# Twelve residual blocks on one core: where residual sums are made, who feeds the scan, how queries are folded

## The reference

```
x  += l0x cross attention (16 heads of 8)          block 1
x  += selective scan of l0a (16 states)            block 2
x  += l0f: 2 of 8 experts                          block 3
x  += l1x cross attention with one key head        block 4
x  += l1a causal self attention                    block 5
x  += l1f: base + one picked adapter               block 6
x  += l2x cross attention over 2048 keys           block 7
x  += norm(l2a gated linear recurrence) * gamma + beta   block 8
x  += l2f: 1 of 16 experts with capacity 40        block 9
x  += norm(l3x: 16 heads of 64, normed q and k, a null key) * g   block 10
x  += l3a self attention, norm, Wfc                block 11
x  += l3f: shared and 4 of 16 experts              block 12
```

## Time and profile before

| | us |
|---|---|
| median of 3 runs | 1161.91 (1161.63 to 1162.94) |
| the profiled execution, its own time | 1163.65 |
| its span, first to last instruction | 1161.9 |
| PE busy | 1075.1 |
| DVE busy | 576.2 |
| ACT busy | 427.0 |
| POOL busy | 312.9 |

### The profile page before, as it was taken

The page is one execution under the profiler, slowest core; times in us unless marked ns, Lnnn a source line. Parts: engine busy times, 40 slices in busy tenths (PEclk is TensorE's granted clock), DMA queues, the critical chain, the costliest instruction groups (busy, mean ns, idle before and its releaser), DMA issues.

```text
span 1161.9 us, 14452 instructions
## 1 busy us (share of the span) xinstructions
PE 1075.1 (93%) x5446; PEld 607.2 (52%) x5446; DVE 576.2 (50%) x1023; ACT 427.0 (37%) x709; POOL 312.9 (27%) x96
## 2 busy tenths in 40 slices
PE   6998798998899889889799999999999999999778
PEld 4554335665744455768564444544454445443654
DVE  2897783236477662344454434444443344343444
ACT  2665513316488633422252233222322332223111
POOL 0000000000000000000016666566746675566000
PEclk9999989988899999999999999999999999999999
DMA  8300000030000020240000000000000000000200
GB/s 334 137 1 1 1 1 1 1 145 1 3 1 1 10 101 1 84 188 1 1 1 18 19 18 20 17 19 18 19 14 19 19 22 14 18 18 5 80 1 10
DMA packets 21372, 40.08 MB, mean 34 GB/s; under 512 B 2496, under 2 KB 18880, under 8 KB 19648
## 3 DMA queue, kind: packets, MB, share of 16 engines
q1 hardware_dynamic: 21312, 39.25, 9.2%
HBM read 38.98 MB, written 0.26 MB: 34 GB/s over the span
## 4 chain that ended last, share of the span: by engine, by line
PE 81%; DVE 10%; ACT 5%; issue 2%; POOL 1%; DMA 0%; POOLq 0%; DVEq 0%; ACTq 0%
PE PSUM L2112 19%; PE PSUM L2116 18%; PE PSUM L1540 10%; PE PSUM L1816 3%; PE PSUM L1827 2%; PE PSUM L1601 2%; PE PSUM L1506 1%; PE PSUM L2023 1%; PE PSUM L1626 1%; PE PSUM L2244 1%; PE PSUM L2159 1%; POOL RSTD L384 1%; PE PSUM L1610 1%; DVE ARENA L985 1%; DVE ST L800 1%
## 5 line engine op out<-in xcount | busy, mean ns | idle before, releaser
L441 POOL TENSOR_TENSOR ARENA<-ARENA 128x2048 f32<-128x2048 f32 x64 | 289.0, 4516 | 175.5 <-ACT ARENA L726 175.5
L1354 DVE TENSOR_TENSOR ARENA<-PSUM,RK 128x512 f32<-128x512 f32 x256 | 175.9, 691 | 280.4 <-PE PSUM L2112 278.5
L2116 PE MATMUL PSUM<-ARENA,CK 128*128 128x512 f32 x512 | 251.2, 593 | 2.1 <-ACT ARENA L726 2.1
L2112 PE MATMUL PSUM<-ARENA,CK 128*128 128x512 f32 x512 | 251.3, 593 | 0.7 <-ACT ARENA L722 0.7
L726 ACT ACTIVATE ARENA<-ARENA,CK 128x2048 f32<-128x2048 f32 x64 | 128.1, 2002 | 311.6 <-DVE ARENA L1354 311.6
L2116 PEld LDWEIGHTS PSUM<-ARENA,CK 128*128 128x128 f32 x512 | 96.7, 190 | 126.4 <-issue 107.9
L2112 PEld LDWEIGHTS PSUM<-ARENA,CK 128*128 128x128 f32 x512 | 96.0, 190 | 117.9 <-issue 96.3
L384 POOL TENSOR_TENSOR RSTD<-VE,MHALF 128x4 f32<-128x4 f32 x15 | 15.1, 1009 | 437.6 <-DVE VE L808 437.6
L1540 PE MATMUL PSUM<-WK,CT 128*128 128x512 f32 x256 | 126.1, 615 | 0.1
L829 DVE TENSOR_REDUCE RK<-SQ 128x8 f32<-128x512 f32 x128 | 84.4, 682 | 28.2 <-ACT SQ L471 27.0
L1513 PE MATMUL PSUM<-WA 128*128 128x128 f32 x584 | 80.8, 293 | 13.3 <-DVE VE L808 10.0
(11 more groups left out here) (395 smaller groups left out, 1199.6 us busy)
## 6 DMA issues: line engine op xcount, KB each, us to landing
CT<-in_ctxT SPq DMA_DIRECT2D x4, 1024.0 KB, 10.3
CK<-in_l0f_experts SPq DMA_DIRECT2D x1, 4096.0 KB, 22.8
CK<-in_ctxk SPq DMA_DIRECT2D x1, 4096.0 KB, 12.5
ARENA<-in_l2f_experts SPq DMA_DIRECT2D x2, 2048.0 KB, 8.9
CK<-in_ctxT SPq DMA_DIRECT2D x64, 64.0 KB, 1.8
CK<-in_ctxr SPq DMA_DIRECT2D x64, 64.0 KB, 1.9
ARENA<-in_l2f_experts SPq DMA_DIRECT2D x1, 3072.0 KB, 14.3
WB<-in_wb SPq DMA_DIRECT2D x1, 2834.5 KB, 11.1
```

Of the source, the lines that this page charges most:

```text
L441: nc.gpsimd.tensor_tensor(LS[b % 2], LS[b % 2], PR[:, k % 2, :], ALU.add)\
L1354: ve.tensor_tensor(PR[:, k % 2, c * 512:(c + 1) * 512].rearrange("p (j n) -> p j n", j=4), PSUM[:, c % 2, :].rearrange("p (j n) -> p j n", ...
L2112: mm(bank(c % 2), CTT[:, k, :], qpb[:, b, c * 512:(c + 1) * 512], start=True, stop=True)\
L2116: return mm(bank(4 + c), CKT[:, k, :], PR[:, k % 2, c * 512:(c + 1) * 512], start=first, stop=final, skip_group_check=True)
```

## The change

1. **Residual sums in the bank.** `put_x_pe` multiplies X by the identity into the output bank, and the block's last products are added on it, in blocks 1, 2, 4, 5, 6 and 11. `norm_dve` reads its statistics from the bank, ACT then copies the bank to X (`keep_x_act`) and signals `x_ready`. The lift of block 1 stands in the heads loop at head 12. Block 3 adds the experts straight to X.
2. **Scan.** For the groups 1 to 3, ACT copies the spread rows of B to SBUF and POOL multiplies them by DTU; two input buffers in place of one; the spreads are in another order.
3. **Start.** An exponential of four numbers stands first on ACT; PE runs four idle products before the first transpose and three of four key groups of the first batch before the queries.
4. **Block 4.** Idle products stand in three more places. In other places their number is lower: after a block's end 4 for 6 before the variance, 5+9 and 6+9 for 6+12 around an output norm, 7 for 11 in block 8, 5 for 9 in block 11.
5. **Norms of outputs** (blocks 8 and 10) are fused with gain and sum into eight instructions, four before and four after POOL's power; block 8's output bias goes into the bank by PE. Blocks 7 and 11 divide and add in four instructions for two.
6. **Last attention, start.** The fold has 8 steps of 8 products in which the two halves of the array's rows alternate, with four pairs of banks; ACT copies one bank and DVE the other. The null scores of batches 1 and 2 stand in the first four key tiles.
7. **Last attention, between batches and end.** The null values are made before they are needed, and added in the midst of the fourth tile's scaling. For the last batch the first eight heads' values are made ahead of the sum over partitions, and the null values are added ahead of the division's denominator.

```diff
@@ scan block: addresses, GpSimd
-        CONV, U, VG, DT, DTU, ZB, EB1 = (ARENA[:, 640 + k * 512:1152 + k * 512] for k in range(7))
+        CONV, ZB, EB1, U, VG, DT, DTU = (ARENA[:, 640 + k * 512:1152 + k * 512] for k in range(7))
-        DBU = ARENA[:, 9472:9472 + 2048]
+        DBU = (ARENA[:, 9472:9472 + 2048], ARENA[:, 0:2048])
+        INPUTS_AT, READS_AT = (0, 4, 12, 20), (8, 16, 24, 28)
             for q in range(4):
+                if q == 1:
+                    nc.gpsimd.wait_ge(sem("l0a_bc_taken"), 1)
+                if q:
+                    for n in range(4):
+                        nc.gpsimd.wait_ge(sem("l0a_b_kept"), PO.due("l0a_b_kept"))
+                        at = DBU[q % 2][:, n * 512:(n + 1) * 512]
+                        nc.gpsimd.tensor_tensor(at, at, DTU, ALU.mult).then_inc(sem("l0a_input"), PO.sends("l0a_input"))
                 nc.gpsimd.wait_ge(sem("l0a_decay"), PO.due("l0a_decay"))
...
@@ ScalarE
+            def keep_x_act(k):
+                nc.scalar.wait_ge(sem("x_counted"), AC.due("x_counted"))
+                act(X[:, :, :].rearrange("p b n -> p (b n)"), bank(k), ACT.Copy).then_inc(sem("x_ready"), AC.sends("x_ready"))
...
+            nc.scalar.wait_ge(sem("halves"), 1)
+            act(SM[:, 1016:1020], MHALF[:, :], ACT.Exp)
             nc.scalar.wait_ge(sem("dma_wa"), AC.due("dma_wa"))
             turn_act(HT)
...
             for q in range(4):
-                due = AC.due("l0a_scan", lag=2)
-                ...
+                if q >= 2:
+                    nc.scalar.wait_ge(sem("l0a_scan"), q - 1)
+                if q:
+                    for n in range(4):
+                        k = INPUTS_AT[q] + n
+                        nc.scalar.wait_ge(sem("l0a_bc"), k + 1)
+                        act(DBU[q % 2][:, n * 512:(n + 1) * 512], bank(SPREAD_BANKS[k % 6]), ACT.Copy)\
+                            .then_inc(sem("l0a_b_kept"), AC.sends("l0a_b_kept"))
...
             for b in range(B):
-                for j in range(4):
+                for j in range(2):
                     nc.scalar.wait_ge(sem("l3x_qp"), AC.due("l3x_qp"))
-                    act(qph[:, b, j // 2, j % 2:8:2, :], bank4(j % 2), ACT.Copy)...
+                    act(qph[:, b, j, 0:8:2, :], bank4(2 * ((2 * b + j) % 4)), ACT.Copy)...
@@ VectorE: norms
-            def norm_dve(src, turned=True, twice=False):
+            def out_norm_dve(src, gain, number):
+                count_dve(src)
+                variance_dve()
+                for b in range(B):
+                    last = ve.scalar_tensor_tensor(out=HN[:, b, :], in0=src[:, b, :], scalar=MV[:, b, 0:1], in1=gain,
+                                                   op0=ALU.subtract, op1=ALU.mult)
+                ...
+                nc.vector.wait_ge(sem("rstd"), DV.due("rstd"))
+                for b in range(B):
+                    last = ve.scalar_tensor_tensor(out=X[:, b, :], in0=HN[:, b, :], scalar=RSTD[:, b:b + 1], in1=X[:, b, :],
+                                                   op0=ALU.mult, op1=ALU.add)
+                last.then_inc(sem("x_ready"), 1)
+            def norm_dve(src, turned=True, twice=False, summed=None, number=0):
+                if summed is None:
+                    count_dve(src)
+                else:
+                    nc.vector.wait_ge(sem("block_out"), DV.due("block_out"))
+                    count_dve(bank4(summed), "x_counted")
+                variance_dve(twice)
+                if summed is not None:
+                    nc.vector.wait_ge(sem("x_ready"), number)
                 nc.vector.wait_ge(sem("rstd"), DV.due("rstd"))
...
-            def tail_dve():
-                nc.vector.wait_ge(sem("block_out"), DV.due("block_out"))
-                ve.tensor_tensor(X[:, :, :], X[:, :, :], bank4(7), ALU.add).then_inc(sem("x_ready"), DV.sends("x_ready"))
...
             for h in range(H):
+                if h == 12:
+                    nc.vector.wait_ge(sem("dma_consts"), DV.due("dma_consts", n=4))
+                    lift_dve(row("l0x_bo"))
...
-            tail_dve()
-            norm_dve(X, twice=True)
+            norm_dve(X, twice=True, summed=7, number=1)
...
@@ VectorE: scan block
-                for n in range(4):
-                    ve.tensor_tensor(DBU[:, at:at + 512], bank(SPREAD_BANKS[(q * 8 + n) % 6]), DTU, ALU.mult)...
+                if q == 0:
...
+                else:
+                    nc.vector.wait_ge(sem("l0a_input"), 4 * q)
...
@@ VectorE: last attention
-            for b in range(B):
-                null_scores(b)
+            null_scores(0)
+            null_scores(3)
+            for b in range(B):
+                for j in range(2):
+                    nc.vector.wait_ge(sem("l3x_qp"), DV.due("l3x_qp"))
+                    ve.tensor_copy(qph[:, b, j, 1:8:2, :], bank4(2 * ((2 * b + j) % 4) + 1))...
             for b in range(B):
                 for k in range(DEEP):
-                    scale(b, k, k)
+                    scale(b, k, k, values_first=b > 0 and k == 3)
+                    if b == 0:
+                        null_scores(1 + k // 2, k % 2)
...
             keep_z(B - 1)
+            null_values(B - 1)
+            add_null_values()
             finish_sums(B - 1)
             finish_values()
             finish_out(B - 1)
-            norm_dve(OAT, turned=False)
-            ve.tensor_tensor(ACC[:, :, :], HN[:, :, :], over(row("l3x_go"), B), ALU.mult)...
-            ve.tensor_tensor(X[:, :, :], X[:, :, :], ACC[:, :, :], ALU.add)...
+            out_norm_dve(OAT, row("l3x_go"), 10)
@@ TensorE
+            def put_x_pe(k):
+                mm(bank(k), ident, X[:, :, :].rearrange("p b n -> p (b n)"), start=True, stop=False, skip_group_check=True)
-            def tail_pe(weight, src=OT):
+            def tail_pe(weight, src=OT, on_x=True):
                 for b in range(B):
+                    ... start=not on_x, stop=True, skip_group_check=on_x)
...
+            stay_busy(4, 1)
             turn_pe()
+            nc.tensor.wait_ge(sem("dma_ctx0"), PE.due("dma_ctx0"))
+            for g in range(1, 4):
+                key_pieces(g, 0)
             nc.tensor.wait_ge(sem("turned_kept"), PE.due("turned_kept"))
...
+            put_x_pe(7)
             turn_pe(ACC)
...
+            spread_inputs(0)
+            stay_busy(2, 1)
+            spread_inputs(1)
+            stay_busy(4, 1)
+            spread_reads(0)
             context_keys_pe(0)
+            stay_busy(14, 1)
             for q in range(4):
+                if q < 2:
+                    spread_inputs(q + 2)
                 for n in range(4):
                     add_state(q, n)
                 if q < 3:
+                    spread_reads(q + 1)
                     context_keys_pe(q + 1)
-            stay_busy(4)
+            put_x_pe(7)
...
-            busy_until_sum(3, 7)
+            busy_until_sum(3, 4)
             busy_until_variance(4, 6, 5)
             turn_pe()
+            stay_busy(2, 1)
             (then the first l1x product, stay_busy(3, 1), the second, stay_busy(3, 1))
...
             for b in range(B):
-                for j in range(4):
+                for j in range(2):
+                    k = 2 * b + j
+                    if k >= 4:
+                        nc.tensor.wait_ge(sem("l3x_qp_kept"), k - 3)
+                        nc.tensor.wait_ge(sem("l3x_qp_taken"), k - 3)
+                    ...
                     for i in range(4):
+                        for half in range(2):
+                            h = 8 * j + 2 * i + half
+                            last = mm(PSUM[:, 2 * (k % 4) + half, i * P:(i + 1) * P],
+                                      w("l3x_WkT")[DH * half:DH * half + DH, (h // 2) * P:(h // 2 + 1) * P],
+                                      QSC[DH * half:DH * half + DH, h // 2, b * P:(b + 1) * P], start=True, stop=True)
...
-            finish_sums(B - 1, SUM_BANK)
+            head_values(range(8))
+            finish_sums(B - 1, 0)
+            head_values(range(8, H)).then_inc(sem("l3x_o"), PE.sends("l3x_o"))
             turn_sums(1)
-            finish_values()
-            stay_busy(8)
+            stay_busy(7, 4)
             finish_turn()
```

279 lines of the change are left out of this document (144 added, 135 removed).

## The result

The changed kernel takes 1138.2 us (median of four executions, 1133.57 to 1139.52) where the kernel before took 1161.88 (1161.63 to 1162.94): a ratio of 0.9767, interval 0.974 to 0.9795; the two medians divide to 0.9796, at the edge of that, so the gain is 2.0 to 2.3%. On a second chip it was 1139.63 (six executions) against 1162.95, 0.9809 (0.9782 to 0.9835).

The account below looks back on a forecast made before the run. PE was taken to bound the kernel (four fifths of the span), with gains only at handovers between blocks; ten terms sum to -27.5, giving 1134.4 us, own range 1129 to 1140, all good ends 1121, all bad 1154.

Parts of the forecast that it names:

- Start: Kernel start: early table load and keys made before the queries end the keys near 17.2, not 19.53; -2.3 us (-3.4 to -1.0).
- Sums in the bank: Ends of six blocks: VectorE's residual add of 0.72 each leaves the path; -3.8 us (-4.3 to -2.5).
- Scan: Block 2: GpSimd makes inputs but excludes VectorE's scan (exclusive case), 9.4 per group; -1.2 us (-8.3 to +1.4).
- Rival A: Block 2: GpSimd runs beside the scan, gaining 8.3 us and not 1.2; total 1127.3, chance 0.27.
- Rival B: Block 4's clock stays at 1.2 GHz and the fold's array halves don't overlap; 3.5 + 5.1 come back, 1143 us, chance 0.20.
- the fold: Last attention's start: eight steps of 16 records at 1.16 or less replace 15.5 us; -6.1 us (-7.2 to -1.0).
- rival C: Some 11 stretches with thinned idle products: clock falls cost about 3.5 us each; slower, 1169 with ten; chance 0.03.
- Block 4: Block 4's first products: added idle products keep the clock from falling to 1.2 GHz; -3.5 us (-4.7 to 0).
- Output norms: Blocks 8 and 10: fused norms save 1.36 each, block 8's bias in the bank 0.72; -3.4 us (-3.8 to -2.4).
- divide and add: Blocks 7 and 11: four instructions for two save 0.28 each; -0.56 us (-0.6 to 0).
- between the batches: Last attention: PE's wait of 1.46 before turning a batch loses 1.1, three times; -3.3 us (-4.4 to 0).
- the end: Last batch: half the value products made before the sums (1.88), plus 0.43 and 0.3; -2.6 us (-3.5 to -1.0).

Follow-up runs that it names:

- the repeated kernel: The changed kernel unaltered, run again on a second chip: 1139.63 us (1137.83 to 1145.78), ratio 0.9809 to the kernel before.

## Why the prediction came out as it did

The forecast was 1134.4 with an own range of 1129 to 1140, and the median is 1138.2. Of the 3.8 that it lies above, 1.8 are in the sum of the steps (27.5 predicted, 25.7 between the two profiles). The other 2.0 are the step from one execution to the median: the execution of before that I worked from stood 1.7 above its median, that of after 0.2 below its own, and I carried the 1.74 over as if it belonged to the kernel. More likely it belonged to how many falls that execution had: in the repeated kernel the time goes with the mean granted clock, 1137.83 at 0.984 and 1145.78 at 0.978. That the sum is off by only 1.8 is partly luck: blocks 1, 3 and 5 fell 3.8 short of their terms, and blocks 2, 4 and 10 went 2.4 beyond theirs. And the bad ends add up to 1155.4, not to 1154: the scan's +1.4, a loss, was counted as a gain.

- **Start: the mechanism failed in the profiled execution.** "What remains after landing is about a quarter of the keys" did not happen there: keys end at 19.65 for 19.53, since the queries stand behind the first context part and then take 5.56. I had read when the fourth part lands and not when the first does, and had let key products that wait for it stand ahead of queries that don't. In the two profiles with queries of 3.6 it did happen: 32 of the 128 records, 1.08, stood behind the last landing, and the keys ended at 16.59 and 17.76. What the profiled execution gained, 1.37 at the 8-row products, is for the most part the gap of 1.08 among the values. In ten profiles of this order block 1 lies between 105.73 and 108.77.
- **Sums in the bank: right** in blocks 1 and 11 by removal (0.67, 0.71). In block 6 it was worth 0.30, and in blocks 2, 4 and 5 it was not measured.
- **Scan: right, the exclusive case.** The predicted cycle was 9.4; the scans start 9.35, 9.07 and 9.08 apart. Four products of 1.27 and a scan of 4.42 would be 9.5, and up to 0.4 is gained at the handover. Of the 1.85 that the two profiles differ by from the first scan's start to the last read's end, the part itself is 0.6; the rest is the stall of 1.27 in the kernel before, which stood behind a fall and which the old code, put back, did not have. So the 1.2 of this term came half from the step that it names and half from a fall that was read as part of the kernel. The bad end, a product ahead of a scan, is what happened twice (5.39, 5.40), without a loss, since the product had to be made anyway.
- **Rival A fell**: GpSimd does not run beside the scan. Rival B fell in both of its halves: no fall at block 4's first products, and halves that overlap. But they overlap in part without alternating too, so the alternation brought 2.0, and the banks and the second engine brought the other 5.3. I had put the fold's cost down to the array, where the chain product, copy, product set it. The term came out 1.2 too small (7.3 for 6.1), as a step is 0.89 and not 1.16.
- **Something like rival C happened in two places.** Block 3 was +0.79 where I had -0.72, block 5 +0.71 where I had -0.72, each by a fall of the clock that costs 1.4 to 1.5. Where no fall comes, block 3 is 69.69, 0.66 below the kernel before, which is its term. That the thinned idle products cause these falls, as the rival has it, no run tests. Block 5's comes and goes between runs (110.07 in the repeat). Block 3's came in eight of the twelve profiles without added idle products; that it is the changed scan block's longer wait of PE was argued here, not shown.
- **Block 4: right**, 3.6 by removal where 3.5 stood. The other 1.4 of the 5.04 are the block's sum in the bank, 0.7 if it is worth what it is in blocks 1 and 11, and a fall at the block's end that the profile of before had (0.57 from 291 to 294) and this one not.
- **Output norms, divide and add, block 8, between the batches, the end**: each within 0.6 of its term. They were only compared before and after, not taken out one by one. PE's wait before a batch is turned fell from 1.46 to 0.20, more than the 1.1 that I had.

## What to carry to other kernels

Before an engine is given work beside another, ask where each operand lies: two of one's inputs in SBUF beside the other's cost a full exclusion here, one of them in PSUM cost nothing. Handing the work over whole brought 0.6; splitting it along that line brought 3.4 more. Where falls of the clock wander from run to run, compare lengths of pieces between several profiles, not two medians, and put no idle product on the word of one.
